# Top-k thresholds from column pairs, window sums on TensorE, and a new interleaving, in a two-layer audio tower

## The reference

```python
h = dct(frames(x))                       # 32 x 626 x 128
h = h + bidirectional_mamba2(norm(h))    # stage 1
h = h + moe(norm(h))                     # stage 2: 8 experts, best 2 per token, 128 -> 512 -> 128, exact gelu
h = h + window_attention(norm(h))        # stage 3: 8 neighbours per token, softmax over them, per channel
h = h + pattern_ffn(norm(h))             # stage 4
```

```python
a = gelu(x @ in_patterns.T)              # 512 per token
a = where(a is among the 64 largest of its row, a, 0)
p = gelu(a @ w1.T)                       # 256 per token; the 128 largest, softmax over them
a = gelu((softmax(top 128 of p) @ values) @ w2.T)   # 512 per token
out = (a where it is among the 64 largest, else 0) @ out_patterns
```

## Time and profile before

| | |
|---|---|
| Time, median of 3 runs | 8142.36 us (8140.66 to 8146.43) |
| Profiled execution, its own time | 8142.98 us |
| Its span, first to last instruction | 8141.2 us |
| Busy, share of the span | DVE 85%, PE 68%, PE weight load 55%, ACT 40%, POOL 37% |
| Granted TensorE clock, mean | 0.800 of full |
| Chain that ended last | DVE 67%, PE 9%, issue 8%, DMA 5%, POOL 5%, ACT 3% |

### The profile page before, as it was taken

The page is one execution under the profiler, slowest core; times in us unless marked ns, Lnnn a source line. Parts: engine busy times, 40 slices in busy tenths (PEclk is TensorE's granted clock), DMA queues, the critical chain, the costliest instruction groups (busy, mean ns, idle before and its releaser), DMA issues.

```text
span 8141.2 us, 109594 instructions
## 1 busy us (share of the span) xinstructions
PE 5529.4 (68%) x31240; PEld 4441.6 (55%) x31240; DVE 6959.1 (85%) x22124; ACT 3232.6 (40%) x7204; POOL 3040.7 (37%) x3192
## 2 busy tenths in 40 slices
PE   6766677776667767667767667767667767667433
PEld 5655555555555555556555556555556555556322
DVE  2378989888989888989888989888989888989887
ACT  2343444433444443344443344433344443344311
POOL 2344443334443433443333443333443333443320
PEclk8887788878788888788877788878788878778755
DMA  2322222222222222222221222222222222222200
GB/s 71 107 79 62 66 85 78 74 65 60 65 85 79 78 62 61 62 85 81 79 64 57 62 84 82 80 62 62 64 77 82 81 65 65 67 67 82 69 2 3
DMA packets 342763, 561.90 MB, mean 69 GB/s; under 512 B 33728, under 2 KB 261792, under 8 KB 341664
## 3 DMA queue, kind: packets, MB, share of 16 engines
q10 hardware_dynamic: 152576, 357.68, 14.2%
q1 hardware_dynamic: 168992, 153.83, 7.3%
q0 software_dynamic: 20480, 41.98, 1.7%
HBM read 484.63 MB, written 68.74 MB: 68 GB/s over the span
## 4 chain that ended last, share of the span: by engine, by line
DVE 67%; PE 9%; issue 8%; DMA 5%; POOL 5%; ACT 3%; ACTq 2%; SPq 1%; DVEq 0%; POOLq 0%
DVE m L1218 15%; DVE work L1221 9%; DVE work L1251 7%; DVE sorted L1248 6%; DVE a L1221 4%; DVE ab L1071 3%; DMA rows<-routed_rows 3%; DVE lg L1173 2%; PE pS L565 2%; PE pD L761 2%; DVE Mt L1082 2%; DMA decay_rows<-dAT 2%; POOL u L387 2%; DVE stats L1030 2%; DVE red L1188 2%
## 5 line engine op out<-in xcount | busy, mean ns | idle before, releaser
L1218 DVE MAX8 m<-work 128x8 f32<-128x512 f32 x1792 | 1143.4, 678 | 1.0
L1221 DVE MATCH_REPLACE8 work<-m,work 128x512 f32<-128x512 f32 x1536 | 1024.8, 674 | 0.0
L565 PE MATMUL pS<-u_fm,wconv_s 128*128 128x315 f32 x3072 | 929.0, 457 | 6.1 <-ACT Cs L849 5.8
L674 PE MATMUL pM<-turned,expert 128*128 128x128 f32 x4352 | 655.2, 297 | 331.7 <-ACT turned L920 327.4
L674 PEld LDWEIGHTS pM<-turned,expert 128*128 128x128 f32 x4352 | 586.0, 206 | 423.6 <-issue 359.9
L565 PEld LDWEIGHTS pS<-u_fm,wconv_s 128*128 128x128 f32 x3072 | 614.2, 205 | 256.3 <-issue 52.8
L907 ACT ACTIVATE hid<-pM,expert 128x128 f32<-128x128 f32 x2176 | 621.2, 370 | 331.6 <-PE pM L674 330.2
L459 POOL TENSOR_TENSOR lg<-lg,red 128x640 f32<-128x640 f32 x256 | 388.5, 1557 | 920.2 <-DVE red L1179 920.2
L685 PE MATMUL pM<-expert,hid 128*128 128x128 f32 x4352 | 672.9, 306 | 0.0
L685 PEld LDWEIGHTS pM<-expert,hid 128*128 128x128 f32 x4352 | 631.6, 223 | 0.0
L599 PE MATMUL pS<-Mt,Xw 121*64 121x121 f32 x3072 | 294.2, 321 | 488.7 <-DVE Mt L1082 486.4
(11 more groups left out here) (243 smaller groups left out, 13975.1 us busy)
## 6 DMA issues: line engine op xcount, KB each, us to landing
expert<-in_experts ACTq DMA_DIRECT2D x544, 578.0 KB, 3.9
ab<-decay_rows SPq DMA_DIRECT2D x384, 230.7 KB
rows<-routed_rows SPq DMA_DIRECT2D x128, 256.0 KB, 5.1
answer_rows<-turned ACTq DMA_DIRECT2D x256, 128.0 KB, 4.0
x_sb<-in_x SPq DMA_DIRECT2D x32, 256.0 KB
out<-hk SPq DMA_DIRECT2D x32, 256.0 KB
routed_rows<-un,slot POOLq DMA_INDIRECT x320, 2.8
rows<-answer_rows,slot POOLq DMA_INDIRECT x320, 2.6
```

Source lines behind the costliest of these rows:

```text
L565: last = nc.tensor.matmul(pS[:, 512 * (n % 3):512 * (n % 3) + HQ], wt, tap(d, i, half * HQ, HQ), start=(j == 0), stop=(j == len(blocks) - 1))
L674: last = nc.tensor.matmul(pM[:, bank(i) + j * P:bank(i) + (j + 1) * P], w1_of(i, j), turned[:, (i + 2) % 4, 1, :], start=True, stop=True)
L1218: link(nc.vector.max(m8[:, i, :], now[i]), len(tiles) - 1)
L1221: link(nc.vector.match_replace(work[i], m8[:, i, :], now[i], GONE), len(tiles) - 1)
```

## The change

1. **Searches on pairs.** `take_top` first takes, per tile, the minimum and the maximum of columns j and j+256 (two TENSOR_TENSOR of 256 columns). It then searches two lists of 256 columns: the 64 largest of the maxima (8 MAX8, 7 MATCH_REPLACE8) and the 32 largest of the minima (4 and 3), and merges them with a minimum over 33 columns per tile and one TENSOR_REDUCE. All ten searches of a clip change so.
2. **Sums on TensorE.** The two trees on POOL go. PE adds the 8 exponentials and the 8 products by matmuls with the identity that accumulate in PSUM, each in two halves of 320 columns (`den_ps`, `val_ps`). ACT copies the first sum to SBUF (`den_sb`), DVE takes the reciprocal and multiplies the two halves out of PSUM. All 8 products are now POOL's; DVE's 4 (L1184) go.
3. **Residuals on TensorE.** h3 and hk are added by further matmuls with the identity, and ACT copies the results (2 copies for h3, 5 for the outputs), where DVE added (L1194, L1198, L1280).
4. **Hint.** The loop is made with `hint_back_edge=True`.
5. **New strings** for all five engines.

Core of the diff:

```diff
+DVE_ORDER = ("342441423442441241441144444444444444444444444444414144411114111141111111114114141314344443414443124")
+ACT_ORDER = ("44443134313433233211341241411111444212211442211111122221144222111214422112112211122222122444144144444321"
+             "41422214112111114214411221111223141411444124111343444433")
...
-            with engine.Fori(last, NB) as b:
+            with nc.Fori(last, NB, engines=[engine.engine], hint_back_edge=True) as b:
...
-            for w in range(4):
-                last = nc.gpsimd.tensor_tensor(red[:, w, :], lg[:, w, :], lg[:, w + 4, :], ALU.add)
...
+            for w in range(AW // 2):
+                last = nc.gpsimd.tensor_tensor(red[:, w, :], lg[:, w, :], v[:, w:w + W], ALU.mult)
+            last.then_inc(G["weighted"].s, 1)
...
+                lo = W // 2 * half
+                for w in range(AW):
+                    last = nc.tensor.matmul(pA[:, 0:W // 2], ident, lg[:, w, lo:lo + W // 2], start=(w == 0), stop=(w == AW - 1))
+                last.then_inc(G["den_ps"].s, 1)
...
+                nc.tensor.matmul(pD[:, 512:512 + P], ident, hk[:, t, :], start=False, stop=True).then_inc(G["fin_ps"].s, 1)
...
+                nc.scalar.copy(hk[:, t, :], pD[:, 512:512 + P]).then_inc(G["out_sb"].s, 1)
...
             def take_top(tiles, src, k, work):
-                nc.vector.memset(tick[:], 0.0)
+                n = len(tiles)
+                upper = [work[i][:, 0:NI // 2] for i in range(n)]
+                lower = [work[i][:, NI // 2:NI] for i in range(n)]
+                for i, t in enumerate(tiles):
+                    nc.vector.tensor_tensor(lower[i], src[:, t, 0:NI // 2], src[:, t, NI // 2:NI], ALU.min)
+                    link(nc.vector.tensor_tensor(upper[i], src[:, t, 0:NI // 2], src[:, t, NI // 2:NI], ALU.max), n - 1)
+                link(nc.vector.memset(tick[:], 0.0))
                 for r in range(k // 8):
                     if r:
                         yield
-                    now = [src[:, t, :] if r == 0 else work[i] for i, t in enumerate(tiles)]
...
+                    lists = [(upper[i], sorted2[:, i, 1, 8 * r:8 * r + 8], k // 8) for i in range(n)]
+                    if r < k // 16:
+                        lists += [(lower[i], sorted2[:, i, 0, 1 + 8 * r:9 + 8 * r], k // 16) for i in range(n)]
+                    for left, top, rounds in lists:
+                        link(nc.vector.max(top, left), len(lists) - 1)
+                    for left, top, rounds in lists:
+                        if r < rounds - 1:
+                            link(nc.vector.match_replace(left, top, left, GONE), n - 1)
+                link(nc.vector.memset(tick[:], 0.0))
+                h = k // 2
+                either = work[0][:, 0:n * (h + 1)].rearrange("p (t n) -> p t n", t=n)
+                link(nc.vector.tensor_tensor(either, sorted2[:, 0:n, 1, k - 1:h - 2:-1], sorted2[:, 0:n, 0, 0:h + 1], ALU.min))
+                nc.vector.tensor_reduce(m8[:, 0:n, 7], either, AX.X, ALU.max)
```

More of the change, by code:

```diff
@@ L463, in pool_stage3 @@
             pool.wait_ge(G["lg_exp"].s, G["lg_exp"](b, 1))
[L464 to L466 removed]
+            for w in range(AW // 2):
+                last = nc.gpsimd.tensor_tensor(red[:, w, :], lg[:, w, :], v[:, w:w + W], ALU.mult)
+            last.then_inc(G["weighted"].s, 1)
             yield
[L468 to L477, removed]
+            pool.wait_ge(G["den_ps"].s, G["den_ps"](b, 2))
             for w in range(AW // 2, AW):
                 last = nc.gpsimd.tensor_tensor(lg[:, w, :], lg[:, w, :], v[:, w:w + W], ALU.mult)
[L480 to L489 removed]
+            last.then_inc(G["weighted"].s, 1)
             yield
@@ L950, in act_stage3 @@
             nc.scalar.activation(lg, lg, ACT.Exp).then_inc(G["lg_exp"].s, 1)
+            for half in range(2):
+                yield
+                act.wait_ge(G["den_ps"].s, G["den_ps"](b, half + 1))
+                lo = W // 2 * half
+                nc.scalar.copy(q[:, lo:lo + W // 2], pA[:, 0:W // 2]).then_inc(G["den_sb"].s, 1)
+            for n, (lo, hi) in enumerate(((0, 4 * P), (4 * P, W))):
+                yield
+                act.wait_ge(G["attT_ps"].s, G["attT_ps"](b, n + 1))
+                nc.scalar.copy(h3[:].rearrange("p t d -> p (t d)")[:, lo:hi], pA[:, 0:hi - lo]).then_inc(G["h3_done"].s, 1)
             for n, (lo, hi) in enumerate(((0, 4 * P), (4 * P, W))):
@@ L1215, in take_top @@
                         yield
-                    now = [src[:, t, :] if r == 0 else work[i] for i, t in enumerate(tiles)]
-                    for i in range(len(tiles)):
-                        link(nc.vector.max(m8[:, i, :], now[i]), len(tiles) - 1)
-                    if r < k // 8 - 1:
-                        for i in range(len(tiles)):
-                            link(nc.vector.match_replace(work[i], m8[:, i, :], now[i], GONE), len(tiles) - 1)
+                    lists = [(upper[i], sorted2[:, i, 1, 8 * r:8 * r + 8], k // 8) for i in range(n)]
[11 more added lines that the diff above has]
+                nc.vector.tensor_reduce(m8[:, 0:n, 7], either, AX.X, ALU.max)
             def select(tiles, done):
@@ L1275, in weigh_pairs @@
                 nc.vector.reciprocal(rsum[:, lo:hi], rsum[:, lo:hi]).then_inc(G["sel2"].s, n)
-            def out(t):
-                yield
-                dve.wait_ge(G["fin_ps"].s, G["fin_ps"](b, t + 1))
-                nc.vector.tensor_tensor(hk[:, t, :], hk[:, t, :], pD[:, 512:512 + P], ALU.add).then_inc(G["out_sb"].s, 1)
             for tiles in groups:
@@ L1297, in dve_stage4 @@
                 dve.wait_ge(G["a3_sb"].s, G["a3_sb"](b, tiles[-1] + 1))
-                for r, _ in enumerate(take_top(tiles, a1, K3, places(0))):
-                    yield
-                    if due and r % 2 == 1:
-                        if due[0] == 0:
-                            yield
-                            dve.wait_ge(G["h3_kept"].s, G["h3_kept"](b, 1))
-                        yield from out(due.pop(0))
+                yield from take_top(tiles, a1, K3, places(0))
                 yield from select(tiles, G["sel3"])
-                due += tiles
-            for t in due:
-                yield from out(t)
+            nc.vector.memset(tock[:], 0.0)
             dve.sem_clear(link4)
```

82 lines of the change are left out of this document (44 added, 38 removed).

## The result

The changed kernel takes 8686.1 us (median of 4 runs, 8677.6 to 8696.9) where the kernel before takes 8141.5 in the same session: a ratio of 1.067 (95% interval 1.065 to 1.069), 545 us more. The forecast was 8325 us, +183, with a range up to 8520. The direction was right, the size a third of the truth. The profiled execution has a span of 8687.5 us at a mean granted TensorE clock of 0.84 of full, against 0.80 before.

What follows compares the result with a forecast made beforehand. DVE was taken as the bound: 206.9 us of work plus waits of 12, 12, 8, 8 and 2.9 make 249.8 a pass against 243.0, +197 over 29 passes, less 15, giving 8325 us; range 7860 to 8520.

Steps and rivals of the forecast that it cites:

- DVE's work: DVE's busy time per clip: 217.5 us less 10.6 saved by searches, sums and residuals, giving 206.9.
- weigh 0: DVE's step after the first cut: it would wait 12 us a pass (9 to 15) for ACT's marks and squares.
- weigh 1: DVE's step after the second cut and one scan: it would wait 12 us a pass (9 to 14) for ACT.
- T3.0: First search over the third activation: DVE would wait 8 us a pass (6 to 10) for three a3 tiles.
- 24 new ones ... I add 0: DVE's new merges and halves, two SBUF inputs each: stalls beside POOL counted as 0, at most 24 us a clip.
- Slots: Point in the pass when expert slots are ready: 46.6 us after the first moments of h3, before 42.8.
- Marks 0: ACT's marks after the first cut: 30.6 us of ACT work plus one 1.3 us PE wait, beginning at 102.
- Marks 1: ACT's next marks: 30.2 us of ACT work from the previous marks, then 4.4, leaving DVE waiting 12 us.
- Filling and draining: Outside the 29 full passes: the searches would save some 15 us in total.
- 5.2 us for the search: Pair searches on DVE: 0.52 us saved per search, 5.2 us a clip.
- ACT keeps up: Rival: table loads fall into ACT's waits for PE; a pass takes 234.5 us, the whole kernel 7880 us; chance 0.30.
- PE becomes the bound: Rival: PE's in-order waits beside 199 us of work make a pass 262 us or more, 8690 us; chance 0.04.

Runs made afterwards that it cites:

- after_bc_first: Changed kernel with SP's four loads of the decay rows moved ahead of the last group of routed rows: 8668.3 us, 1.0637 of before.
- one_table_after: Changed kernel with the projections' Silu replaced by Gelu, so they share the expert tiles' table (output differs): 8181.1 us, 1.0057 of before.
- old_orders_sq: All new code in the old strings with new pieces set in, moments of h one search round earlier, PE's sq ahead of oT2: 8089.8 us, 0.9945.
- one_table_before: Kernel before with the projections' Silu replaced by Gelu (output differs), on the slower chip: 8468.8 us, 0.9989 of before.
- after_old_search: Changed kernel with the 512-wide search put back, measured twice: 9346.1 us (1.1035) on the slower chip, 9117.6 us (1.1212) on the other.
- search_only: Kernel before with only the new search over column pairs, old strings and plain loop: 8404.6 us, 1.0332 of before.
- search_moved: Kernel before with the pair search, and moments of h, gate and choice one search round earlier; slower chip: 8602.6 us, 1.0153.

## Why the prediction was off

The mechanism was right: the new ACT string has 34 table loads a clip (35 forecast), DVE has no cover ahead of its waits, and these eat more than the savings. The hint removed its wait, MAX8 of 256 is 0.412 us (0.41), a six-list round 4.33 us (6 x 0.720). PE grew by 20 us a clip, at a clock of 0.84 and not at the equal one that the forecast named, and hid nearly all of them. The pass came out 261.2 instead of 249.8, by these terms:

| us a pass | forecast | measured |
|---|---|---|
| DVE's work | 206.9 | 209.5 |
| weigh 0 | 12 (9 to 15) | 17.2 |
| weigh 1, with the scan ahead of it | 12 (9 to 14) | 2.8 + 7.6 |
| T3.0 | 8 (6 to 10) | 10.3 |
| end of the pass | 8 (6 to 10) | 7.8 |
| small waits and gaps | 2.9 | 6.1 |

- *DVE's work.* "24 new ones ... I add 0" was wrong in an unforeseen way. The new instructions hardly meet POOL, but the new order sets POOL's subtraction beside three old routing instructions (L1151 twice, L1154 once, 1415 ns where it was 199), 3.7 us a pass, and frees L1254, 1.05. That makes 2.6. The searches' instructions (L1212 to L1221 before, L1228 to L1246 now) cover 94.9 us of a pass before and 89.4 now, 5.5 less where 5.2 was forecast, though the halves take 2.2 us for three tiles, not 1.9. DVE worked 217.0 us in a pass before (5643.0 / 26), not 217.5. These two are 0.8 the other way, and as much was not traced.
- *Slots* came at +50.8 (from the prediction's zero, here 4186.25) instead of +46.6, mostly by these 3.7 us, and the first expert copy at +74.4 instead of +70.4. The 23.6 us between are as forecast by luck. The rows had landed some 3 us before; the tile stood behind the third a2, on PE and on ACT, of which the prediction says that it "is there by then". The third a2 hangs on the selects of T1.0, which come right behind the slots on DVE and were late by as much.
- *Marks 0* came at +110.1 instead of +102.3: 4.0 from the first tile, and 3.8 because the stretch from there took 35.7 us instead of 30.6 + 1.3. The walk through ACT had "one wait of 1.3" for PE; the trace has six, 8.7 us together, while ACT's own work came out 3.6 below the 30.6. The cut came 4.5 late too, so weigh 0 waits 15.9 us in the pass shown, 3.9 more than forecast, and 17.2 on the mean of 25 passes, above the range's 15. This is the main step that failed: a chain of two engines was summed as one engine's work. The counts of it, nine loads and six gelu tiles, were right.
- *Marks 1 and the scan.* 10.4 together, 1.6 below the forecast. That the first scan would wait for SP was not seen, and it cost next to nothing, as `after_bc_first` shows.
- *T3.0.* In the pass shown 13.7 us from weigh 1's start to the third a3 (13 forecast) against 4.65 of DVE's work (4.5): a wait of 9.05. The mean over passes is 10.3, just above the forecast's end of 10.
- *Small waits.* vare and Xw behind PE, 2.7 us a pass, were left out without a reason, though Xw waited for PE before as well (2.2 a pass).
- *Filling and draining* cost 545 - 528 = +17 instead of -15: the searches' savings do not appear where the same strings run with stages missing. This was not tested.
- *5.2 us for the search.* As DVE's work it was right (5.5). Its worth in time was never that number.

The upper end, 8520, let all waits reach their ends but gave the pass no late slots and no waits for PE. The rival "ACT keeps up" is refuted: marks 0 is 10.5 us late. "PE becomes the bound" has nearly the measured time, 8690, but by another cause: PE is busy 191 of 261 us, DVE's long waits are for ACT, and `one_table_after` saves 505 us with the same matmuls.

The version to keep is the smallest of these changes: the hint alone, 8029.9 us, 0.9873 of before. Of the variants with all the new code `old_orders_sq` is the best (0.9945), and both beat the kernel before.

## What to carry to other kernels

Where strings fix the order, a piece of code has no price of its own; test it in the old strings first, and look at when each of its rounds ends, not only at its sum. A chain between two engines that work in turn is walked with both engines' waits in it, and what stands ahead of its first step is paid in full. A wait with another behind it is worth what is left after the second. And compare the granted clock and PE's busy time of two kernels before all of a difference is put down to waits.

## What was unexpected of the hardware

- The loop's hint gave 3.6 us a pass (105 us in all) on a loop of 29 passes, nearly all of the "issue" wait at its start.
- A table load took 1283 ns in every group and kernel here. Where ACT has room it costs nothing: `one_table_before` has 284 instead of 555 and its ratio is 0.9989 (0.9974 to 1.0004). In a chain 804 fewer gave 505 us. The Trainium skill ("ScalarE: Activation LUTs", What ACT_TABLE_LOAD costs) gives 1283 ns for the load, with which every run agrees, and a drain that makes it 2.66 us. The drain was not seen: in ACT's timeline of the pass above a load starts within 0.02 us of the end of the activation or copy before it, unless ACT waited there, and the next activation about 0.015 us behind the load.
- In three places a DVE instruction with two SBUF inputs took about as long as one POOL instruction of 640 columns beside it, whatever its own size: 40 columns 1459 ns (197 free), 256 columns 1.75 us (0.42 free), 130 columns 1346 ns (296 free). Moving POOL's work moved the stall to other instructions.
- Two chips differ by 4% on the same kernel (8141 and 8473 us, at granted clocks of 0.80 and 0.78), and not evenly: `after_old_search` is 1.1035 of before on one and 1.1212 on the other. So `search_only` and `search_moved` can't be compared by time.
- The mean granted clock went from 0.77 to 0.86 over these kernels, and PE's busy time for the same matmuls went with it: 5967 us at 0.857 (`one_table_after`), 6163 at 0.840, 6295 at 0.822, 6403 at 0.816.
